# Stage 2 of a two-layer graph network: TensorE's transposes of the node rows replaced by VectorE's 32x32 block transposes and an exchange through DRAM

## The reference, cut to what matters

```python
h = jnp.maximum(_layernorm(x), 0.0)
# first network
msg = relu(h[src] + edge_attr)
g = h + zeros_like(h).at[dst].add(msg)
z = g @ W1 + b1                              # 256 -> 512
z = (z - mean(z, 0)) / sqrt(var(z, 0) + EPS) * bn_gamma + bn_beta
y = relu(z) @ W2 + b2                        # 512 -> 256
# then norms of y over the whole graph and per channel, relu, and
x1 = x + (h + relu(norms(y)))
# second network
h1 = jnp.maximum(_layernorm(x1), 0.0)
agg = segment_sum((h1 @ M)[src], dst, 50000)
out = x1 + relu(h1 @ W + agg)
```

## Time and profile before

| what | value |
|---|---|
| time of three runs | 2449.05 us median (2446.25 to 2455.07) |
| span of the profiled execution | 2446.4 us |
| the median run less that span | 2.65 us |
| stage 2, first hidden matmul to last output matmul | 461.8 to 1622.5 us |
| steps of stage 2 between | 98 |

### The profile page before, as it was taken

How to read it: one execution, slowest core, us unless ns; L and a number is a source line. 1 busy time by engine, 2 the same in 40 slices (tenths; PEclk the granted TensorE clock), 3 DMA queues, 4 the chain that set the end, 5 groups by cost and what they waited for, 6 DMA issues and landing times. The chain is left out here.

```text
span 2446.4 us, 48745 instructions
## 1 busy us (share of the span) xinstructions
PE 2354.5 (96%) x12271; PEld 2013.5 (82%) x12271; DVE 2052.5 (84%) x5707; ACT 1713.3 (70%) x3449; POOL 1708.5 (70%) x1599
## 2 busy tenths in 40 slices
PE   7999998799999999999999999979999999989997
PEld 6888886588888888888888888858989888969996
DVE  8999997598888888888888888967777777749996
ACT  6999997466666666666666666638888888846664
POOL 5777777577767667767766666717777777767774
PEclk8999999899999999999999999999999999999999
DMA  8888995323444444444444344349999999765662
GB/s 257 283 278 275 278 277 170 124 58 127 152 150 158 163 151 147 146 146 166 153 147 145 145 164 154 141 173 405 405 411 413 413 413 413 294 197 162 173 177 88
DMA packets 242978, 531.73 MB, mean 217 GB/s; under 512 B 53856, under 2 KB 141177, under 8 KB 231442
## 3 DMA queue, kind: packets, MB, share of 16 engines
q1 hardware_dynamic: 182434, 459.36, 51.2%
q0 software_dynamic: 59808, 70.24, 10.2%
q10 hardware_dynamic: 592, 0.54, 0.1%
HBM read 340.23 MB, written 286.84 MB: 256 GB/s over the span
## 5 line engine op out<-in xcount | busy, mean ns | idle before, releaser
L1020 POOL DMA_INDIRECT ar<-sum_table,idx x392 | 462.3, 1179 | 177.6 <-issue 96.5
L1067 ACT ACTIVATE r<-pair,bnC,bnA 128x512 f32<-128x512 f32 x392 | 305.9, 781 | 380.2 <-PE pair L1268 377.7
L1471 POOL DMA_INDIRECT x1d_table<-x1r,slot x392 | 383.8, 979 | 139.8 <-issue 123.9
L1175 DVE CAST rH<-r 128x512 fp32r<-128x512 f32 x392 | 391.0, 997 | 97.7 <-ACT r L1067 97.7
L1694 PE MATMUL pair<-Ws,h1T 128*128 128x256 f32 x1568 | 358.7, 382 | 8.9 <-DVE orr L1602 7.4
L1694 PEld LDWEIGHTS pair<-Ws,h1T 128*128 128x128 f32 x1568 | 290.2, 190 | 52.1 <-issue 14.3
L1284 PE MATMUL bank<-rH,W2h 128*128 128x512 f32 (+1 forms) x784 | 305.6, 390 | 1.8 <-ACT yr L1081 1.8
L1284 PE MATMUL bank<-rL,W2h 128*128 128x512 f32 (+1 forms) x784 | 305.7, 390 | 0.0
L1284 PE MATMUL bank<-rH,W2l 128*128 128x512 f32 (+1 forms) x784 | 305.0, 389 | 0.0
L836 PE MATMUL bank<-hr 128*128 128x257 f32 (+1 forms) x1568 | 274.2, 329 | 9.6 <-ACT hr L535 9.6
L1184 DVE TENSOR_TENSOR rL<-r,rH 128x512 fp32r<-128x512 f32 x392 | 271.1, 691 | 13.5
(11 more groups left out here) (239 smaller groups left out, 5234.1 us busy)
## 6 DMA issues: line engine op xcount, KB each, us to landing
xr<-in_x SPq DMA_DIRECT2D x186, 512.0 KB, 3.9
xy_kept<-xy_table SPq DMA_DIRECT2D x57, 1024.0 KB, 20.7
x_table<-x1r SPq DMA_DIRECT2D x97, 512.0 KB, 19.8
out<-orr SPq DMA_DIRECT2D x97, 512.0 KB
xy_table<-xr SPq DMA_DIRECT2D x89, 512.0 KB, 2.6
xy_table<-yr SPq DMA_DIRECT2D x89, 512.0 KB, 3.3
xyr<-xy_table SPq DMA_DIRECT2D x32, 1024.0 KB, 21.0
sum_table<-e_tot SPq DMA_DIRECT2D x99, 128.0 KB, 4.5
```

The costliest lines, as they stand in the source:

```text
L1020: pool.indirect_dma_start(ar[0:p, s, j, :], None, sum_table[:, :], bass.IndirectOffsetOnAxis(ap=idx[0:p, s, j:j + 1], axis=0), bounds_chec ...
L1067: act.activation(r32[:, m, 0:n], z_ps[m][:, 0:n], ACT.Relu, bias=bnC[:, m:m + 1], scale=bnA[:, m:m + 1]).then_inc(r_kept, 1)
L1175: dve.tensor_copy(rH[:, s, m, 0:n], r32[:, m, 0:n]).then_inc(rh_kept, 1)
L1471: pool.indirect_dma_start(x1d_table[:, :], bass.IndirectOffsetOnAxis(ap=slot[0:p, part, s * T + j:s * T + j + 1], axis=0), x1r[0:p, s, j, ...
```

## The change

Groups 0, 1 and 97 are turned by PE as before (`by_tensor`). For the other 95 groups:

- DVE transposes `ar` by blocks of 32x32 into `blocks`, the first half of which was W2's staging tile, 128x1024 in one instruction (`turn_blocks`). Within each 32x32 block rows and channels are exchanged; the blocks themselves stay in the 32 partitions from which they came.
- SP writes `blocks` to a DRAM table by four DMAs of 128 KB, one for each quarter of the partitions, in runs of 512 bytes, and reads it back by one DMA of 512 KB in runs of 4 KB into a staging tile, where each partition holds one channel. Two tiles take turns: W and M's, and W1's staging tile.
- `keep_high` and `keep_low` read that tile in place of PSUM, with the columns put in order by their access pattern.
- h, the add, the turn and the x load run three groups ahead of the hidden layer instead of two; DVE's prologue now includes add(2) and turn_blocks(2), and ACT's the four pieces of h(2).
- y has two pairs of banks, the second being the one in which PE's transposes were kept; output(k) waits for keep_y(k-2) instead of keep_y(k-1).
- In DVE's step keep_low(k+1) moves from the front to behind the second subtraction, and add(k+3) and turn_blocks(k+3) follow it. In ACT's step keep_high(k+1) moves behind hidden(k, 0).
- POOL waits for turn_blocks(k-2) and not for PE before it clears `ar`, and takes its ids straight from `ids`, without the copy.
- All 98 steps are written out on every engine.
- W and M are loaded at the start of stage 3 on SP's queue, behind its first four loads, and the first `h1 @ W` waits for them.

```diff
+        blocks = W2s[:].rearrange("p a b -> p (a b)")
+        staged = [WM[:].rearrange("p a b c -> p (a b c)"), W1s[:].rearrange("p a b -> p (a b)")]
-        hT_ps, z_ps, y_ps = pair[0], [...], bank
+        y_ps = [[pair[0][:, c, :] for c in range(KC)], [bank[c][:, :] for c in range(KC)]]
+            def turned_part(k, c, n):
+                if by_tensor(k):
+                    return hT_ps[:, c, 0:n]
+                return staged[k % 2][:, c * GC:(c + 1) * GC].rearrange("p (q t n) -> p t q n", q=QUADS, t=T)
...
+                def load_turned(k):
+                    if not exists(k) or by_tensor(k):
+                        return
+                    if k == 3:
+                        sp.wait_ge(q_made, 1)
+                    sp.wait_ge(ht_out[k % 2], 16 * QUADS * exchanges(k))
+                    after(sp, tl_kept, k - 1)
+                    sp.dma_start(staged[k % 2], ht_table[k % 2].rearrange("b p c q n -> (b p) (c q n)")
+                                 ).then_inc(ht_in[k % 2], 16)
...
+                def store_blocks(k):
+                    if not exists(k) or by_tensor(k):
+                        return
+                    sp.wait_ge(blocks_made, blocks_until(k))
+                    after(sp, ht_in[k % 2], 16 * (exchanges(k) - 1))
+                    for q in range(QUADS):
+                        sp.dma_start(ht_table[k % 2, :, :, :, q, :].rearrange("b p c n -> p c b n"),
+                                     blocks[q * SQ:(q + 1) * SQ, :].rearrange("p (c b n) -> p c b n", c=KC, b=QUADS)
+                                     ).then_inc(ht_out[k % 2], 16)
...
+                for k in range(3):
+                    load_rows(k)
+                for k in range(-2, NG + 3):
+                    load_turned(k + 2)
+                    load_rows(k + 5)
+                    store_rows(k + 2)
+                    store_y(k - 2)
+                    clear_slots(k - 1)
+                    store_blocks(k + 3)
...
+                def turn_blocks(k):
+                    if not exists(k) or by_tensor(k):
+                        return
+                    dve.wait_ge(h2_done, k + 1)
+                    if k > 2:
+                        dve.wait_ge(ht_out[(k - 1) % 2], 16 * QUADS * exchanges(k - 1))
+                    dve.transpose(blocks.rearrange("p (b t n) -> p t b n", b=KC * QUADS, t=T),
+                                  ar[:, k % AU, :, :].rearrange("p t (b n) -> p t b n", n=SQ)).then_inc(blocks_made, 1)
...
-                def step(at):                        # DVE
-                    stats(back(at, 2), 0)
-                    keep_low(back(at, -1))
-                    stats(back(at, 2), 1)
-                    high(at, 0)
-                    low(at, 0)
-                    high(at, 1)
-                    low(at, 1)
-                    add(back(at, -2))
+                def step(k):                         # DVE
+                    stats(k - 2, 0)
+                    high(k, 0)
+                    low(k, 0)
+                    stats(k - 2, 1)
+                    high(k, 1)
+                    low(k, 1)
+                    keep_low(k + 1)
+                    add(k + 3)
+                    turn_blocks(k + 3)
...
-                def step(at):                        # PE
-                    turn(back(at, -1))
+                def step(k):                         # PE
+                    if k + 1 < NG - 1:
+                        turn(k + 1)
                     for m in range(HC):
-                        hidden(at, m)
-                        output(back(at, 1), m)
+                        hidden(k, m)
+                        if m == 0 and k + 1 == NG - 1:
+                            turn(k + 1)
+                        output(k - 1, m)
...
+                sp.dma_start(Ws, W.rearrange("(k p) n -> p k n", p=P)).then_inc(w_loaded, 16)
+                sp.dma_start(Ms, M.rearrange("(k p) n -> p k n", p=P)).then_inc(w_loaded, 16)
```

More of the change, by code:

```diff
@@ L30 @@
 CA = CH + 16
+SQ = 32
+QUADS = P // SQ
 def back(at, lag):
@@ L893, in turn_over @@
             for _ in range(times):
-                pe.matmul(target, ident[:], Ws[:].rearrange("p a b -> p (a b)"), start=True, stop=True)
+                pe.matmul(target, ident[:], W1s[:, 0, :], start=True, stop=True)
         next_phase()
@@ L927, in gnn_kernel @@
         h2_done = sem("h2_done")
+        blocks_made = sem("blocks_made")
+        ht_out = [sem(f"ht_out{s}") for s in range(2)]
+        ht_in = [sem(f"ht_in{s}") for s in range(2)]
         t2_made = sem("t2_made")
@@ L963, in _, with nodes_of @@
+            def turned_part(k, c, n):
+                if by_tensor(k):
+                    return hT_ps[:, c, 0:n]
+                return staged[k % 2][:, c * GC:(c + 1) * GC].rearrange("p (q t n) -> p t q n", q=QUADS, t=T)
+            def nodes_of(part, k):
+                return part if by_tensor(k) else part.rearrange("p (t q n) -> p t q n", q=QUADS, t=T)
             @block.sync
             def _(sp):
-                def step(at):
[L967 to L993, removed]
@@ L1035, in _, with gather @@
-                rounds(pool, step, WHOLE - 2, NU, NPEEL, NG - WHOLE + 2 + 2)
+                def gather(k):
+                    if not exists(k):
+                        return
+                    s = k % AU
+                    p, n = group_shape(k)
+                    if k >= AU:
+                        if by_tensor(k - AU):
+                            pool.wait_ge(t2_made, turns_until(k - AU))
+                        else:
+                            pool.wait_ge(blocks_made, blocks_until(k - AU))
+                    pool.nop(nofuse=True)
+                    pool.memset(ar[0:p, s, 0:n, :], 0.0).then_inc(a2_clear, 1)
+                    pool.wait_ge(a2_clear, k + 1)
+                    pool.nop(nofuse=True)
+                    for j in range(n):
+                        pool.indirect_dma_start(ar[0:p, s, j, :], None, sum_table[:, :],
+                                                bass.IndirectOffsetOnAxis(ap=ids[0:p, k * T + j:k * T + j + 1], axis=0),
+                                                bounds_check=ET * P - 1, oob_is_err=False
+                                                ).then_inc(a2_in[s], 16)
+                    if k == 1:
+                        pool.memset(blank[:], 0.0).then_inc(blank_made, 1)
@@ new lines, in residual @@
+                def residual(k):
+                    if not exists(k):
+                        return
+                    p, n = group_shape(k)
+                    pool.wait_ge(h2n_done, k + 1)
+                    pool.nop(nofuse=True)
+                    pool.tensor_tensor(xbuf(k)[0:p, 0:n, :], xbuf(k)[0:p, 0:n, :], hr[0:p, k % AU, 0:n, :],
+                                       ALU.add).then_inc(xh2_done, 1)
+                for k in range(NG + 2):
+                    gather(k)
+                    residual(k - 2)
@@ L1310, in _ @@
                 last.then_inc(q_made, 1)
-                turn((0, 0, 0, NU))
+                turn(0)
                 pe.wait_ge(var_made, 1)
-                rounds(pe, step, WHOLE - 2, NU, 1, NG - WHOLE + 2 + 1)
+                for k in range(NG + 1):
+                    step(k)
         weights.close()
```

243 lines of the change are left out of this document (136 added, 107 removed).

## The result

The changed kernel takes 2470.3 us (median of four runs, 2465.6 to 2472.6) against 2449.8 us before: a ratio of 1.0076 (95% interval 1.0059 to 1.0093), slower by 0.8%. I had forecast 2393 us and a range of 2366 to 2460. The profiled execution is the one of 2465.58 us, with a span of 2463.9. The direction was wrong, and rivals 2 and 3 were nearer than the forecast.

What follows compares the result with a forecast made beforehand. PE was taken to bound stage 2 at 11.77 us per group; 95 x (11.77 - 11.10) saves 63.7 us, less 6.3 (start) and 1.3 (stage 3), 56 us: forecast 2393 us, range 2366 to 2460.

Steps and rivals of the forecast that it cites:

- rival 2: Stage 2: DVE's add is held by POOL's addition in each group, pace stays 11.77 us, 2457 us; chance 0.14.
- rival 3: Stage 2: keep_low, now with two SBUF operands, is held by POOL's addition, 12.39 us per group, 2515 us; chance 0.14.
- PE's floor without its transposes: Stage 2: PE alone needs 10.88 us per group once its transposes go, 0.89 less than 11.77.
- The transpose at 1.2 us: Stage 2, DVE: one block transpose of 128x1024 per group takes 1.2 us, taken from the add's rate.
- DVE's unheld work at 9.15 us: Stage 2: DVE's work per group without holding, 7.95 us, becomes 9.15 us with the transpose.
- If add goes first: Stage 2: POOL's addition then lies beside transpose and next cast; the transpose takes 1.2 us of holding, DVE's group 10.2 us.
- three groups in four at PE's floor: Stage 2: three groups in four at 10.88 us and one at 11.77 give a pace of 11.10 us; a judgement.
- the 2.25 I took: Stage 2: time per group in which DVE's casts are held, 2.25 us; with all of it DVE needs 11.40 us.
- Rival 4: Stage 2: the exchange through DRAM is late, stores landing in twice 4.5 us, 11.85 us per group, 2464 us; chance 0.08.
- It is hidden, with about 3 us to spare: Stage 2 exchange: stores and next transpose need 19.2 us of the 22.2 us that two groups give.
- The second pair of y banks: Stage 2, PE's wait for ACT's copy of y: at most 4 us of gain, counted as nothing.
- The start: Start of stage 2: PE's step 1 begins at 481.6 us in place of 475.3, a cost of 6.3 us.

Runs made afterwards that it cites:

- no_pool_add: Changed kernel with POOL's addition of h to x in stage 2 left out, a one-column memset in its place: 2365.0 us, ratio 0.9655.
- low_from_psum: Changed kernel with keep_low's first operand read from PSUM, so one operand in SBUF, and one pair of y banks: 2477.3 us, ratio 1.0116.
- no_exchange: Changed kernel without the four stores and the load of each group's turned tile, and without the waits for them: 2470.8 us, ratio 1.0090.
- timed_add: Changed kernel with POOL's addition for group k-1 waiting for DVE's add of that group, and DVE's statistics behind the transpose: 2366.5 us, ratio 0.9665.
- pool_only: Changed kernel with POOL's addition for group k-1 waiting for DVE's add of that group, DVE's order kept: 2415.5 us, ratio 0.9856.
- late_clear_pool: pool_only with POOL clearing ar only when DVE has taken the cast that follows the block transpose: 2381.3 us, ratio 0.9721.

## Why the prediction was wrong, point by point

- PE's floor without its transposes, 10.88 us: right, 10.87 in three kernels.
- The transpose at 1.2 us: right, 1.245. The reshape rate that the Trainium skill gives (Vector Engine (DVE) Microarchitecture Reference, 3.8 The reshape front-end and per-opcode configuration) agrees as far as the rows go: 1024 columns in 1.245 us, where the add, with one result per lane and column, takes 1.228.
- DVE's unheld work at 9.15 us: 9.30 measured.
- keep_low from SBUF costs no more by itself: right, 0.683 us in no_pool_add.
- The step that failed is "If add goes first, POOL's addition lies beside the transpose and the next cast; the transpose takes 1.2 us of the holding, and DVE's group is 10.2 us", with the ratio of three groups in four at PE's floor that I set on it. Add had gone first in 31 of 90 groups and not in three of four, and the whole transpose lay beside POOL's addition in only 19. Even there the cast was still held by 1.8 us, which makes 9.30 + 1.8 = 11.1 us for DVE, above PE's floor and not the 10.2 of the forecast, because POOL's clearing now follows its addition at once and holds the cast too. In the kernel before the clearing waited for PE, over 1 us behind the addition. Net, the holding costs 2.46 us per group, more than the 2.25 I took for the case where all of it stays. With 9.30 + 2.46 DVE is at 11.76 us, above PE's 10.88, in the place of the 11.10 that I forecast; 95 times the 0.83 between 11.93 and 11.10 is 79 us, and the forecast was 77 us off.
- Rivals 2 and 3 both took place, in a third of the groups each. Rival 3's mechanism was right, its price was not: a held keep_low takes the place of a held add, and the pace is no different (low_from_psum). Rival 4 fell with no_exchange.
- "It is hidden, with about 3 us to spare": hidden in the changed kernel, but the spare time isn't there. At PE's floor, where the forecast lay, DVE and ACT wait for the exchange in most groups (timed_add), and PE just doesn't.
- "The second pair of y banks ... I count it as nothing; it is at most 4 us" failed too. It is hidden in the changed kernel, where DVE is the bound, but worth 31 us where PE is. I had read the small wait in the earlier trace rows without asking what covered it: the transposes that the change removes.
- The start: step 1 at 481.6 us predicted, 482.07 measured:

```profile
482.07 1.22 PE L1340 MATMUL pair<-tH,W1h 128*128 128x512 f32 x2 [12.04 <-DVE tL L1220]
```

- W and M in stage 3: 1.3 us predicted, none seen (571.1 against 571.7 us).
- Not tried: why 0.37 us of lead on the record lose the port and 0.96 us win it, and so what sets the shares of the collisions.

## What to carry to other kernels

A second engine that is held up while it has room costs nothing, and becomes the price of any work that is moved onto it: before moving work, take the engine's busy time with the held part listed apart, and ask which instruction the holder will lie on afterwards. Then place the holder: a change of DVE's order and one semaphore wait, so that POOL's addition lies over DVE instructions with one SBUF operand, turned a loss of 0.8% into a gain of 3.4%. DVE's order alone gave 3.3%, POOL's edit alone 1.4%. And an edit that removes work from the bounding engine also removes that work's cover: the wait for the y banks was free only because PE was turning rows meanwhile.

## What the runs showed of the hardware that I had not expected

- POOL's memset, which reads nothing, holds a DVE cast: the casts that it holds end 0.28 us behind its end (1102.87 against 1102.59 in pool_only), and moving it away gave 34 us. A subtraction of rL, which has two operands in SBUF, is not held by it: in the changed kernel one starts at 1117.40, within the clearing of 1117.17 to 1118.25, and takes its usual 0.69 us. Of add and keep_low no such overlap was seen. A clearing that is moved behind a cast holds the next one (late_clear_pool).
- An add that is recorded as starting 0.36 to 0.40 us ahead of POOL's addition is held until it ends, as the add of the earlier trace rows was, and so are adds with 0.5 us in low_from_psum; with a lead of 0.96 us it runs freely, and POOL's addition is then recorded as 2.50 us long in place of 2.40.
- The block transpose of float32, 128x1024 in 32x32 blocks with a permuted output, takes 1.245 us, alone or beside POOL.
